# VectorE sums the first long chunk's probabilities from its second step on, and ScalarE copies the context out of PSUM

## What is computed

```python
# x: (8, 1024, 256), 8 heads of 32, DEPTH = 5, hidden 768
paths = sigmoid(x @ Wp + bp)                      # (B, H, T, 5)
agree = pq * pk + (1.0 - pq) * (1.0 - pk)
sim = cumprod(agree, axis=-1).sum(axis=-1) / 5    # causal mask
attn = softmax(sim);  ctx = attn @ (x @ Wv);  y = ctx @ Wo
x = layernorm(x + y)
x = layernorm(x + (silu(x @ wg.T) * (x @ wu.T)) @ wd.T)   # int weights / 127
```

## Time and profile before

| | |
|---|---|
| median of 3 runs | 862.34 us (860.69 to 864.26) |
| the profiled execution's own time | 864.53 us |
| its span, first to last instruction | 862.8 us |
| TensorE's granted clock, mean | 0.980 of full speed |
| busy: TensorE | 795.2 us, 92% |
| busy: VectorE | 613.8 us, 71% |
| busy: ScalarE | 456.7 us, 53% |
| busy: GpSimd | 294.5 us, 34% |

### The profile page before, as it was taken

One profiled execution on the slowest core, in us unless ns is written; L12 is line 12 of the kernel. 1 busy time (PEld: TensorE's weight loads), 2 busy tenths in 40 slices (PEclk: granted clock), 3 DMA queues, 4 the chain that ended last, 5 costly groups with the idle time before them and its releaser, 6 DMA issues.

```text
span 862.8 us, 14316 instructions
## 1 busy us (share of the span) xinstructions
PE 795.2 (92%) x5506; PEld 389.5 (45%) x5506; DVE 613.8 (71%) x1101; ACT 456.7 (53%) x721; POOL 294.5 (34%) x266
## 2 busy tenths in 40 slices
PE   5199899999999999999999999999999998999885
PEld 4043346443554536444454436444464444444253
DVE  1936776679666795677766796667966777667966
ACT  2155664656446573655545574565636565465422
POOL 0011262243413462152522444134622526234424
PEclk9689999999999999999999999999999999999989
DMA  6651436006530237106350055302370063400001
GB/s 234 167 126 50 101 81 152 35 1 147 132 114 1 63 87 194 50 1 140 85 161 7 2 145 147 98 2 76 96 172 1 1 148 88 109 1 1 25 1 51
DMA packets 44358, 71.02 MB, mean 82 GB/s; under 512 B 3584, under 2 KB 21248, under 8 KB 44288
## 3 DMA queue, kind: packets, MB, share of 16 engines
q1 hardware_dynamic: 44288, 70.07, 31.1%
HBM read 53.28 MB, written 16.78 MB: 81 GB/s over the span
## 4 chain that ended last, share of the span: by engine, by line
PE 55%; DVE 24%; issue 9%; ACT 6%; DMA 3%; POOL 1%; SPq 1%; DVEq 0%; POOLq 0%; ACTq 0%
PE slot L804 9%; PE misc L882 9%; PE ctx_ps L824 8%; PE misc L780 8%; PE misc L870 7%; PE misc L847 6%; DVE acc L548 6%; DVE work L648 5%; PE den_ps L830 5%; ACT probs L464 4%; DVE x L631 3%; DVE acc L545 2%; DVE x1T_lo L638 2%; PE misc L789 1%; DVE ctx_raw L558 1%
## 5 line engine op out<-in xcount | busy, mean ns | idle before, releaser
L464 ACT ACTIVATE probs<-slot 128x1024 f32<-128x1024 f32 (+3 forms) x384 | 290.2, 808 | 301.7 <-PE slot L804 271.9
L398 POOL TENSOR_SCALAR_AFFINE_SELECT probs<-probs 128x512 f32<-128x512 f32 x128 | 147.0, 1150 | 223.6 <-ACT probs L464 223.4
L804 PE MATMUL slot<-query_stack,key_stack 128*128 128x512 f16 (+3 forms) x768 | 161.8, 331 | 17.4 <-DMA query_stack<-phi_dram 15.2
L412 POOL TENSOR_TENSOR work<-work 128x512 f16<-128x512 f32 x96 | 116.1, 1209 | 176.3 <-ACT work L482 176.3
L824 PE MATMUL ctx_ps<-probs,vz_sb 128*32 128x512 f32 (+3 forms) x1536 | 163.4, 498 | 5.0 <-DVE ctx_raw L558 2.6
L870 PE MATMUL misc<-x1T_hi,w_parts 128*128 128x512 f16 x358 | 135.8, 379 | 8.6 <-DVE x1T_lo L638 6.0
L804 PEld LDWEIGHTS slot<-query_stack,key_stack 128*128 128x128 f16 x768 | 56.1, 98 | 178.9 <-issue 122.1
L870 PE MATMUL misc<-x1T_lo,w_parts 128*128 128x512 f16 x358 | 135.7, 379 | 0.0
L548 DVE TENSOR_TENSOR acc<-acc,probs 128x1536 f32<-128x1536 f32 (+3 forms) x64 | 106.1, 1658 | 1.8 <-POOL probs L398 1.6
L648 DVE SCALAR_TENSOR_TENSOR work<-work,misc 128x512 f32<-128x512 f32 x89 | 60.7, 682 | 60.5 <-ACT work L476 60.5
L882 PE MATMUL misc<-w_parts,work 128*128 128x256 bf16 x720 | 85.2, 276 | 4.4 <-POOL work L412 4.0
(11 more groups left out here) (78 smaller groups left out, 752.8 us busy)
## 6 DMA issues: line engine op xcount, KB each, us to landing
key_stack<-phi_dram SPq DMA_DIRECT2D x64, 256.0 KB, 5.9
query_stack<-phi_dram SPq DMA_DIRECT2D x64, 256.0 KB, 6.6
xT_sb<-in_xT_dram SPq DMA_DIRECT2D x8, 1024.0 KB, 5.0
x_sb<-in_x_dram SPq DMA_DIRECT2D x8, 1024.0 KB, 5.7
out_dram<-x SPq DMA_DIRECT2D x15, 512.0 KB, 3.9
phi_dram<-phi_hi SPq DMA_DIRECT2D x16, 256.0 KB, 2.0
phi_dram<-phi_lo SPq DMA_DIRECT2D x16, 256.0 KB, 2.3
work<-in_wgT_dram SPq DMA_DIRECT2D x1, 768.0 KB, 8.4
```

The costliest lines, as they stand in the source:

```text
L398: pool.affine_select(out=tile, in_=tile, compare_op=ALU.is_ge, fill=0.0, base=0, pattern=[[0, 4], [1, P]], channel_multiplier=-1).then_inc ...
L412: pool.tensor_tensor(hid_lo[:, n % M1, :], hid[:, n % HSLOTS, :], hid_hi[:, n % M1, :], ALU.subtract).then_inc(hid_lo_ready, 1)
L464: act.activation(probs[:, s % P_SLOTS, 2 * p:2 * p + 2, off:CH], slot[p][:, :, off:CH], ACT.Exp).then_inc(slot_drained[p], 1)
L804: mm = pe.matmul(slot[p][:, k, off:CH], key_stack[:, h, P * j:P * (j + 1)], query_stack[:, h, CH * c + off:CH * (c + 1)], start=True, stop ...
```

## The change

The table entry of chunk 2 goes from 3 to 1, so that VectorE adds from the chunk's second tile (step 9) on. The additions in a batch go from 10 to 12 and the products with ones (L830) of steps 9 and 10 go away. And the copy of `ctx_ps` moves from VectorE's normalising to ScalarE, at the same place of the plan.

```diff
-    ADD_FROM = {2: 3, 3: 1}
+    ADD_FROM = {2: 1, 3: 1}
...
+            def context_out(b, q):
+                Q = NQ * b + q
+                act.wait_ge(pv_done, NS * b + LAST[q] + 1)
+                if Q >= 1:
+                    act.wait_ge(ctxT_ready, Q)
+                act.activation(ctx_raw[:, :], ctx_ps[:, :], ACT.Copy).then_inc(ctx_out, 1)
+
...
+                elif what == "normalise":
+                    context_out(*n)
...
                 dve.wait_ge(pv_done, NS * b + LAST[q] + 1)
                 if q in ADD_FROM:
                     dve.wait_ge(acc_used, NA * b + list(ADD_FROM).index(q) + 1)
-                if Q >= 1:
-                    dve.wait_ge(ctxT_ready, Q)
-                dve.tensor_copy(ctx_raw[:, :], ctx_ps[:, :]).then_inc(ctx_out, 1)
                 dve.transpose(den_turned[:, :, :].rearrange("p a n -> p (a n)"), den_ps[:, :]).then_inc(den_out, 1)
```

## The result

| | before | changed |
|---|---|---|
| median of 4 runs | 862.39 us | 873.96 us (870.43 to 874.48) |
| span of the profiled execution | 862.8 us | 872.1 us |
| TensorE's granted clock, mean | 0.980 | 0.964 |

What follows compares the result with a forecast made beforehand. It took VectorE to set the pace in stretches (steps 12 to 14, 17 to 23), though TensorE is 92% busy. Terms -4.3 - 2.7 - 0.6 + 4.9 + 1.5 = -1.2 us gave 861.1 us, range 855 to 867.

Steps and rivals of the forecast that it cites:

- TensorE's saving: Products with ones removed before step 13: 13.9 us of TensorE's time, put at nothing because TensorE only waits longer in step 14.
- The collisions: Steps 12 to 14: additions and GpSimd hold each other up, +0.7 us a batch, +4.9 us in seven, bounds 2.2 and 7.1.
- The prediction's own sign of being wrong: Wrong if the second-residual-to-x1-split stretch grows over 1.0 us or shrinks, or step 7's gate doesn't come earlier.
- The first batch: Step 12 of the first batch: the second addition holds back the reciprocal root and so L631; +1.5 us once.
- The copy in steps 5 and 6: Without the copy on VectorE, step 7's gate starts 0.6 us earlier in batches 1 to 7: -4.3 us.
- The copy in steps 17 to 23: VectorE never pauses there, so the next hidden value starts 0.45 us earlier; -2.7 us over six batches.
- In steps 1 and 9 the copy was put at nothing: Normalising in steps 1 and 9 isn't waited for, since TensorE is busy with other work; worth nothing.
- No collisions to speak of: Rival, 15%: GpSimd's instructions fall beside L648 and L656, which let them run alongside; 855.2 us.
- ScalarE's copy is late: Rival, 5%: the exponentials behind ScalarE's copy delay the scores in steps 6 and 17, cancelling the copy's gains; 868.7 us.
- The root goes first: Rival, 14%: in step 12 GpSimd's reciprocal root gets SBUF before the second addition, which starts 1.01 us later; 867.8 us.
- TensorE's time counts: Rival, 4%: the removed products' 13.9 us come off, with the copy's 4.3; about 844 us.
- The -0.6 for the copy in the last batch: Steps 17 to 23 of the last batch, where ScalarE waits for these additions: the copy's move gains 0.6 us.

Runs made afterwards that it cites:

- fill_in_wait: The changed kernel plus three groups of needless products with zeros inside TensorE's wait at the turning of x1 in step 14; 867.71 us, ratio 1.0053.
- fill_in_place: The changed kernel plus needless products with zeros where the removed products with ones of steps 9 and 10 stood; 860.69 us, ratio 0.9978.
- fill_one: The changed kernel plus one group of needless products with zeros inside TensorE's wait in step 14; 870.02 us, ratio 1.0085.
- skip_fourth: The changed kernel with the tile of step 11 summed by TensorE, so no addition stands in step 12; 851.77 us, ratio 0.9871.
- copy_chunk2: The kernel before with only chunk 2's copy (steps 17 and 18) moved to ScalarE, additions as before; 859.86 us, ratio 0.9966.
- copy_only: The kernel before with the copy moved to ScalarE, additions as before; 857.17 us, ratio 0.9937.
- late_split: The changed kernel with the split of hidden value 10 moved from step 13 to step 14, behind the turning of x1; 872.4 us, ratio 1.0112.
- from_third: The changed kernel with chunk 2's additions starting at its third tile, one addition more than the kernel before; 860.63 us, ratio 0.9964.

## Why the prediction was wrong

**TensorE's saving, "TensorE only waits longer there. So I put this saving at nothing".** This is the step that failed, and twice over. The first cost has no term in the sum: after the longer wait, 2.90 us, TensorE ran at the lower clock. fill_in_wait measures it: 873.96 - 867.71 = 6.2 us, and by the periods 0.43 + 0.99 + 1.06 + 0 + 0.88 in the middle, 1.06 in the seventh and 2.2 in the last stretch, less 0.4 in the first. Of the 2.2 only a part belongs to this wait: the windows of the changed kernel show the lower clock there from 790 to 794 us, behind it, but also at 820 to 824 and more of it from 838 to 844, behind waits for GpSimd of 2.20 and 3.38 us, which fill_in_wait has as well. The prediction saw the wait coming ("1.5 us or more") and priced it as idle time only. The second cost is in the sum under the wrong name: the collisions of step 13 were written down as a price of the additions, while they came only where TensorE was 1.7 us earlier. fill_in_place has the additions without that, and they cost 0.03 us a batch; with it the stretch grows by 1.03 us, 7.2 us in seven batches.

The clock's fall was also a rule that could have been a rival. The Trainium skill (TensorE: Matmul & The Clock Gate, Why this matters for your kernels) advises against long pauses of TensorE between bursts of matmuls, since the clock then drops. The trace agrees in six batches, with 0.57 after 2.90 us, and not in the seventh, with 1.00 after 2.91. I did not weigh it.

**The collisions, +4.9 us with bounds 2.2 and 7.1.** Followed rightly and sized low. The root was stretched to 3.02 us (predicted about 3) and still came in time, L637 lost 0.42 (0.4), the next addition got back 0.19 (0.2). The open question was who comes first at the third addition. GpSimd did, by 0.07 us, in every batch whose wait was 2.9 us, and the stretch lost 1.03 us, the upper bound of 1.0, not 0.7. Times seven that is 7.2 us. No batch can show the middle of the two cases. In the changed kernel the order was the same all seven times; but the plan alone doesn't fix it, since in fill_one VectorE was first in one batch of seven, by 0.03 us, behind a batch in which the clock had fallen. The prediction's own sign of being wrong, that the stretch grows by more than 1.0 us, came true by a hair (1.03). Without the clock's fall the time is 867.71 us (fill_in_wait), just above the range of 855 to 867; the clock's fall makes the rest.

**The first batch, +1.5.** It is +2.81 (in skip_fourth, without an addition in step 12, +0.92). From the second residual (79.26, before 80.43) to the split it took 12.13 us in place of 9.93, +2.2. The late root held L637 back by 2.0 us, as predicted. L637 itself took 2.33 in place of 1.71, beside masks, 0.6 more, for which I had 0.4 as a possibility only, and the gap of 0.53 ahead of the next addition gave its part back. The remaining 0.6 lies behind the split, where the windows show a clock of 0.83, 0.50 and 0.82 from 92 to 98 us, and 1.00 in the kernel before; its share was not measured apart.

**The copy in steps 5 and 6, -4.3.** It is -0.19 a batch, -1.3 in all. VectorE did come 0.6 us earlier, but into the mask of step 6, which had cost nothing as long as it lay beside the reciprocal and the transposes. The wait ahead of the gate fell to 0.65 us and not to the 0.2 that was expected. The prediction searched steps 12 and 13 for collisions and not this place.

**The copy in steps 17 to 23, -2.7.** Right in its cause and nearly in its size: from the weigh of step 13's tile (390.13, changed 396.11) to the hidden value of step 17 the changed kernel needs 12.48 us in place of 12.94, -0.46 against 0.45 predicted. Of that 0.38 a batch reach the period, by copy_chunk2, or 2.3 us in six batches. In steps 1 and 9 the copy was put at nothing. That holds in the middle batches, but not in step 1 of the last batch, where the kernel before has TensorE waiting 1.74 us for `ctx_raw` (at 733.13 us): copy_only's seventh period is 1.20 us shorter, 0.63 more than its middle ones.

**The rivals.** "No collisions to speak of" is refuted by the rows of 3.24 and 1.79 us. "ScalarE's copy is late" didn't happen: its copy starts with VectorE's transpose at 353.44 and the exponentials 0.49 us later. "The root goes first" didn't either: the addition started 0.11 us after the start of L609 and 0.14 before the root. Their times, 868 to 869 us, were nearer than mine, for another reason. "TensorE's time counts" got 4% and was false for this change, yet skip_fourth shows that a part of it is to be had, 0.84 us a batch, where VectorE's gap in step 12 stays open.

**The sum with what was measured** is -5.3 for the copy as a whole (copy_only) + 7.2 + 2.8 + 6.2 = +10.9 us, against 873.96 - 862.39 = +11.57. The agreement says no more than that nothing large is missing: the difference of two medians is good to 1 or 2 us. The -0.6 for the copy in the last batch was not measured apart.

**What stays open.** What decides whether the clock falls after a given wait: the same 2.9 us brought it down in six batches and not in the one from 455 to 556 us, and shorter waits were followed by it too, four of the six of 1.9 us in fill_one and four of the seven of 1.94 us in late_split.

## What to carry to other kernels

Taking work off an engine that then waits is not free: it moves everything that this engine releases, and what was ordered harmlessly may now collide, while the longer wait itself may cost TensorE its clock. Before a saving is put at nothing, follow each instruction that becomes ready earlier, on every engine, and ask whom it now comes ahead of. And where a wait can't be avoided, try where the saved work is best given back: the fastest version here differs from the changed kernel in a single tile, which TensorE sums instead of VectorE, and is 1.3% faster than before where that one is 1.2% slower.

## What the runs showed of the hardware

- VectorE and GpSimd held each other up in these pairs until the instruction that was first had ended, whoever was second. An addition of 128x2048 took 3.24 instead of 2.29 us behind a GpSimd instruction of 1.16 us that began 0.07 us earlier; `ctxT` 1.10 instead of 0.69 behind a mask of 0.64; and even a reciprocal root over 128x4 elements took 3.02 instead of 1.01 behind an addition. So an operand of four elements a partition was held up like one of 512. The Trainium skill (SBUF — State Buffer, SBUF: two separate sides) states this as an exclusive lock that the first to start keeps for its whole instruction, and these rows agree with it. L656, which reads the bank `misc` in PSUM, kept its 0.75 us beside a GpSimd split of 1.16 (before, at 383.55 and 383.38).
- L637, a tensor_scalar with one SBUF tensor as input, was held up too: 1.79 instead of 1.38 us for four, beside a mask of 0.64.
- After waits of 2.9 us TensorE's granted clock was 0.57 and 0.58 in the two windows of 2 us, in six batches of seven, which cost up to 1.06 us a middle batch. After the waits of 1.9 us in fill_one and late_split it fell eight times in thirteen. After waits of 1.09 us and less in from_third, fill_in_place and skip_fourth it never did in a middle batch.
- Needless products in such a wait made the kernel 6.2 us faster (873.96 to 867.71).
